# Storing the last four row pairs from partitions 96, 100, 104 and 108, one partition at a time, with sixteen staging slots and x in loads of eight pairs

## The reference

```python
bilinear = jnp.einsum('bie,ied->bid', feature, weight)
out = jnp.einsum('bid,bjd->bij', bilinear, feature)
```

## Time and profile before

| | |
|---|---|
| median of 3 runs | 1463.5 us (1458.56 to 1463.85) |
| the profiled execution's own time | 1465.03 us |
| its span, first to last instruction | 1463.2 us |
| TensorE busy | 1330.3 us (91%) |
| VectorE busy | 985.6 us (67%) |
| ScalarE busy | 934.7 us (64%) |
| moved by DMA | 438.55 MB, mean 300 GB/s |

### The profile page before, as it was taken

One profiled execution on the slowest core, in us unless ns is written; L12 is line 12 of the kernel. 1 busy time (PEld: TensorE's weight loads), 2 busy tenths in 40 slices (PEclk: granted clock), 3 DMA queues, 4 the chain that ended last, 5 costly groups with the idle time before them and its releaser, 6 DMA issues.

```text
span 1463.2 us, 39805 instructions
## 1 busy us (share of the span) xinstructions
PE 1330.3 (91%) x16192; PEld 1225.6 (84%) x16192; DVE 985.6 (67%) x1877; ACT 934.7 (64%) x1100; POOL 306.5 (21%) x518
## 2 busy tenths in 40 slices
PE   7999998999999988998999989999889999999974
PEld 7988888898888888888888878888879888889853
DVE  0667676667666766767676766766676767676785
ACT  5666666666666666766666666666666666666643
POOL 0112122222121212212221212222222222222221
PEclk9999999999999999999999999999999999999998
DMA  9799999999999999999999999999999999999998
GB/s 274 236 301 295 322 313 298 317 285 319 312 286 297 293 308 314 299 322 283 316 304 312 296 292 323 290 314 302 308 312 288 322 304 298 322 300 317 265 262 267
DMA packets 264788, 438.55 MB, mean 300 GB/s; under 512 B 51616, under 2 KB 250272, under 8 KB 252320
## 3 DMA queue, kind: packets, MB, share of 16 engines
q1 hardware_dynamic: 240032, 422.78, 88.9%
q0 software_dynamic: 24576, 13.24, 6.8%
HBM read 108.13 MB, written 327.68 MB: 298 GB/s over the span
## 4 chain that ended last, share of the span: by engine, by line
DMA 42%; PE 34%; SPq 9%; DVE 9%; ACT 3%; issue 3%; ACTq 0%; DVEq 0%; POOLq 0%
DMA out_dram<-staging 42%; PE ps L272 15%; PE ps L256 13%; SPq L194 8%; PE ps L244 6%; DVE staging L305 4%; ACT staging L305 3%; DVE win L357 2%; DVE win L365 1%; DVE win L364 1%; SPq L182 1%; DMA x<-feature_dram 1%; SPq L189 0%; ACT xt L318 0%; ACT bl L328 0%
## 5 line engine op out<-in xcount | busy, mean ns | idle before, releaser
L272 PE MATMUL ps<-win,bl 64*100 64x200 f32 x8192 | 771.2, 338 | 59.4 <-DVE staging L305 41.0
L272 PEld LDWEIGHTS ps<-win,bl 64*100 64x100 f32 x8192 | 697.8, 207 | 120.6 <-issue 64.2
L305 ACT COPY staging<-ps 100x800 f32<-100x800 f32 x683 | 548.2, 829 | 328.9 <-PE ps L272 169.8
L227 POOL DMA_DIRECT2D out_dram<-staging x512 | 305.8, 597 | 1146.1 <-ACT staging L305 910.4
L305 DVE COPY staging<-ps 100x800 f32<-100x800 f32 x341 | 335.2, 983 | 234.2 <-PE ps L272 206.8
L357 DVE COPY win<-xt 128x400 f32<-128x400 f32 x512 | 278.5, 544 | 208.7 <-PE ps L272 155.1
L256 PE MATMUL ps<-xt,w 64*64 64x128 f32 x6400 | 371.0, 271 | 15.2 <-DVE staging L305 9.9
L256 PEld LDWEIGHTS ps<-xt,w 64*64 64x64 f32 x6400 | 348.5, 133 | 33.4 <-issue 20.5
L328 ACT COPY bl<-ps 128x1024 f32<-128x1024 f32 (+1 forms) x208 | 202.3, 981 | 153.7 <-PE ps L256 153.7
L244 PE MATMUL ps<-ident,x 128*128 128x128 f32 x1600 | 205.0, 282 | 44.0 <-DVE staging L305 20.1
L244 PEld LDWEIGHTS ps<-ident,x 128*128 128x128 f32 x1600 | 179.2, 144 | 69.1 <-issue 60.4
## 6 DMA issues: line engine op xcount, KB each, us to landing
out_dram<-staging SPq DMA_DIRECT2D x1024, 300.0 KB, 7.6
x<-feature_dram SPq DMA_DIRECT2D x80, 1024.0 KB, 9.7
x<-feature_dram SPq DMA_DIRECT2D x16, 1280.0 KB, 9.7
out_dram<-staging POOLq DMA_DIRECT2D x512, 25.0 KB, 5.8
w<-weight_dram SPq DMA_DIRECT2D x24, 128.0 KB, 6.0
w<-weight_dram SPq DMA_DIRECT2D x2, 64.0 KB, 4.6
```

The costliest lines, as they stand in the source:

```text
L227: nc.gpsimd.dma_start(out_v[FA:FH, PB * (s - 1):PB * (s + 1), :], staging[FA:FH, slot - 1:slot + 1].rearrange("p s b h j -> p (s b) (h j)" ...
L272: last = nc.tensor.matmul(tile[0:FH, h, F * b:F * (b + 1)], row_of_bl(n, R * k + PB * i + b)[64 * h:64 * h + 64], win[64 * h:64 * h + 64, ...
L305: copy(staging[:, slot, :, :, :].rearrange("p b h j -> p h b j"), tile_of("scores", s)[0:FH, :, 0:PB * F].rearrange("p h (b j) -> p h b j" ...
```

## The change

- **The rest on SyncE.** Pairs 96 to 99 are kept on partitions 96, 100, 104 and 108 (`TOP` is 109, the places between hold zeros, written once by three memsets on VectorE for which ScalarE waits at the start). After every eighth set SyncE issues four transfers, each of one partition x sixteen batches. GpSimd stores nothing more.
- **Sixteen staging slots** in place of ten; the rest's semaphore covers eight slots.
- **x in loads of eight pairs.** Two buffers of one group each, so two buffers hold one bundle where they held two. The loads that go out two sets behind a bundle's transposes are for the very next bundle.
- **Three window slots** in place of four.
- **Seven bundles**, the last of four pairs, slipped in at other sets.
- Scores and staging copies run over 109 partitions in place of 100.

```diff
-    OSLOTS = 10
-    WSLOTS = 4
+    OSLOTS = 16
+    WSLOTS = 3
     FA = FH // 16 * 16
-    BUNDLES = [range(2 * v, 2 * v + 2) for v in range(NG // 2 - 1)] + [range(NG // 2 * 2 - 2, NG)]
+    APART = 4
+    TOP = FA + APART * (FH - FA - 1) + 1
+    REST = 16 // PB
+    BUNDLES = [range(2 * v, min(2 * v + 2, NG)) for v in range((NG + 1) // 2)]
...
-    transposed_at = {3: 0, 9: 1, 19: 2, 29: 3, 40: 4, 50: 5}
-    weighed_at = {9: 0, 19: 1, 29: 2, 40: 3, 50: 4, 59: 5}
+    transposed_at = {3: 0, 10: 1, 19: 2, 28: 3, 37: 4, 46: 5, 54: 6}
+    weighed_at = {10: 0, 19: 1, 28: 2, 37: 3, 46: 4, 54: 5, 59: 6}
...
-        x = sbuf("x", [128, XSLOTS, 2 * E * XPAIRS])
+        x = sbuf("x", [128, XSLOTS, 16 * E])
-        staging = sbuf("staging", [FH, OSLOTS, PB, 2, F])
+        staging = sbuf("staging", [TOP, OSLOTS, PB, 2, F])
...
             def load_x(at):
-                n, v = at // NV, at % NV
+                n, u = at // NG, at % NG
                 if at >= XSLOTS:
-                    before = at - XSLOTS
-                    sp.wait_ge(transposed, before // NV * NG + BUNDLES[before % NV][-1] + 1)
+                    sp.wait_ge(transposed, at - XSLOTS + 1)
...
+            def store_rest(s):
+                first = s - REST + 1
+                half = slice(first % OSLOTS, first % OSLOTS + REST)
+                for i in range(FH - FA):
+                    p = FA + APART * i
+                    sp.dma_start(out_v[FA + i:FA + i + 1, PB * first:PB * (s + 1), :],
+                                 staging[p:p + 1, half].rearrange("p s b h j -> p (s b) (h j)")
+                                 ).then_inc(rest_written[first % OSLOTS // REST], 16)
...
                     store(n * SETS_B + s)
-                    if s - 2 in transposed_at:
-                        at = (n + 1) * NV + transposed_at[s - 2] + XSLOTS
-                        if at < BLOCKS * NV:
-                            load_x(at)
+                    if s % REST == REST - 1:
+                        store_rest(n * SETS_B + s)
+                    if n + 1 < BLOCKS and s - 2 in transposed_at:
+                        for u in BUNDLES[transposed_at[s - 2]]:
+                            if (n + 1) * NG + u + XSLOTS < BLOCKS * NG:
+                                load_x((n + 1) * NG + u + XSLOTS)
...
-            for s in range(1, BLOCKS * SETS_B, 2):
-                store_rest(s)
...
-                        last = nc.tensor.matmul(tile[0:FH, h, F * b:F * (b + 1)],
+                        last = nc.tensor.matmul(tile[0:TOP, h, F * b:F * (b + 1)],
...
-                engine.wait_ge(rest_written[slot // 2], 16 * used)
+                engine.wait_ge(rest_written[slot // REST], 16 * (FH - FA) * used)
...
+            act.wait_ge(margin_zero, 3)
...
+            nc.vector.memset(bl[:, FA:TOP, :], 0.0).then_inc(margin_zero, 1)
+            nc.vector.memset(bl[:, 0:FA, FA:TOP], 0.0).then_inc(margin_zero, 1)
+            nc.vector.memset(bl[:, TOP:NB, FA:TOP], 0.0).then_inc(margin_zero, 1)
```

More of the change, by code:

```diff
@@ L40, in feature_interaction @@
     TILES = 4
-    OSLOTS = 10
-    WSLOTS = 4
+    OSLOTS = 16
+    WSLOTS = 3
     FA = FH // 16 * 16
-    BUNDLES = [range(2 * v, 2 * v + 2) for v in range(NG // 2 - 1)] + [range(NG // 2 * 2 - 2, NG)]
+    APART = 4
+    TOP = FA + APART * (FH - FA - 1) + 1
+    REST = 16 // PB
+    BUNDLES = [range(2 * v, min(2 * v + 2, NG)) for v in range((NG + 1) // 2)]
     NV = len(BUNDLES)
-    XPAIRS = max(sum(GROUPS[u] for u in bundle) for bundle in BUNDLES)
     assert 2 * E == 128 and B % NB == 0 and FH % 8 == C and R == 2 * PB
-    assert PB * F <= 512 and OSLOTS % 2 == 0
+    assert PB * F <= 512 and OSLOTS % REST == 0 and SETS_B % REST == 0 and TOP <= NB
     feature_v = feature.rearrange("b f e -> b (f e)")
@@ L53, in feature_interaction @@
     out_v = out.rearrange("b (m h) j -> m b (h j)", h=2)
-    transposed_at = {3: 0, 9: 1, 19: 2, 29: 3, 40: 4, 50: 5}
-    weighed_at = {9: 0, 19: 1, 29: 2, 40: 3, 50: 4, 59: 5}
+    transposed_at = {3: 0, 10: 1, 19: 2, 28: 3, 37: 4, 46: 5, 54: 6}
+    weighed_at = {10: 0, 19: 1, 28: 2, 37: 3, 46: 4, 54: 5, 59: 6}
     assert sorted(transposed_at.values()) == sorted(weighed_at.values()) == list(range(NV))
     assert all(s // 2 + WSLOTS - 1 >= min(2 * BUNDLES[v][-1] + 1, LINES - 1) for s, v in transposed_at.items())
-    assert all(PB * (s + 1) >= min(8 * BUNDLES[v][-1] + 8, FH) for s, v in weighed_at.items())
+    assert all(PB * (s + 1) >= (8 * BUNDLES[v][-1] + 8 if v + 1 < NV else TOP) for s, v in weighed_at.items())
     uses = []
@@ L115, in feature_interaction @@
         out_written = [sem(f"out_written{i}") for i in range(OSLOTS)]
-        rest_written = [sem(f"rest_written{i}") for i in range(OSLOTS // 2)]
+        rest_written = [sem(f"rest_written{i}") for i in range(OSLOTS // REST)]
+        margin_zero = sem("margin_zero")
         block = ctx.enter_context(nc.Block())
@@ L143, in group_of_bl @@
         def group_of_bl(n, u):
-            if n % 2 == 0:
-                return bl[:, 8 * u:8 * u + GROUPS[u], :]
-            return bl[:, :, 8 * u:8 * u + GROUPS[u]]
+            places = slice(8 * u, 8 * u + GROUPS[u]) if 8 * u < FA else slice(FA, TOP, APART)
+            return bl[:, places, :] if n % 2 == 0 else bl[:, :, places]
         def row_of_bl(n, b):
-            return bl[:, b, 0:FH] if n % 2 else bl[:, 0:FH, b]
+            return bl[:, b, 0:TOP] if n % 2 else bl[:, 0:TOP, b]
         def staged_by_dve(s):
@@ L176, in load_x @@
             def load_x(at):
-                n, v = at // NV, at % NV
+                n, u = at // NG, at % NG
                 if at >= XSLOTS:
-                    before = at - XSLOTS
-                    sp.wait_ge(transposed, before // NV * NG + BUNDLES[before % NV][-1] + 1)
-                first, size = 16 * E * BUNDLES[v][0], 2 * E * sum(GROUPS[u] for u in BUNDLES[v])
+                    sp.wait_ge(transposed, at - XSLOTS + 1)
+                size = 2 * E * GROUPS[u]
                 sp.dma_start(x[:, at % XSLOTS, 0:size],
-                             feature_v[n * NB:(n + 1) * NB, first:first + size]
+                             feature_v[n * NB:(n + 1) * NB, 16 * E * u:16 * E * u + size]
                              ).then_inc(x_loaded[at % XSLOTS], 16)
@@ L195, in store @@
                              ).then_inc(out_written[slot], 16)
[L197 to L201, removed]
+            def store_rest(s):
[6 more added lines that the diff above has]
+                                 ).then_inc(rest_written[first % OSLOTS // REST], 16)
+            for u in range(NG + XSLOTS):
+                load_x(u)
+                if u < NG:
+                    load_w(u)
             for n in range(BLOCKS):
@@ L211, in _ @@
                 sp.wait_ge(out_written[slot], 16 * uses)
-                if slot % 2:
-                    sp.wait_ge(rest_written[slot // 2], 16 * uses)
+                if slot % REST == REST - 1:
+                    sp.wait_ge(rest_written[slot // REST], 16 * (FH - FA) * uses)
         @block.gpsimd
@@ L236, in transposes @@
             def transposes(n, u):
[L237 to L241, removed]
+                at = n * NG + u
+                pe.wait_ge(x_loaded[at % XSLOTS], 16 * (at // XSLOTS + 1))
+                wait_tile(pe, "transposes", at)
                 for c in range(GROUPS[u]):
-                    m = 8 * (u - BUNDLES[v][0]) + c
                     last = nc.tensor.transpose(transpose_tile(n, u)[:, c // C, :, c % C, :],
-                                               x[:, at % XSLOTS, 2 * E * m:2 * E * (m + 1)], ident[:])
+                                               x[:, at % XSLOTS, 2 * E * c:2 * E * (c + 1)], ident[:])
                 last.then_inc(transposed, 1)
@@ L303, in stage @@
                 engine.wait_ge(out_written[slot], 16 * used)
-                engine.wait_ge(rest_written[slot // 2], 16 * used)
+                engine.wait_ge(rest_written[slot // REST], 16 * (FH - FA) * used)
             copy(staging[:, slot, :, :, :].rearrange("p b h j -> p h b j"),
-                 tile_of("scores", s)[0:FH, :, 0:PB * F].rearrange("p h (b j) -> p h b j", j=F)
+                 tile_of("scores", s)[0:TOP, :, 0:PB * F].rearrange("p h (b j) -> p h b j", j=F)
                  ).then_inc(staged, 1)
```

## The result

The changed kernel takes 1839.2 us (median of 4 runs, 1837.0 to 1845.1) against 1461.5 before (median of 4, the three of the first table among them): a ratio of 1.259, 95% interval 1.255 to 1.263. The forecast was 1493 with a range of 1400 to 1560. The direction was right, the size far off: +378 us where +30 were forecast.

A forecast was written before the change was run, and what follows sets the result against it. TensorE and the DMA engines were taken as nearly full together in the overlapped blocks. Fifteen blocks +33, last block -7 and block 0 +4 made +30 on the median of 1463.5: about 1493 us, range 1400 to 1560.

The forecast's parts named there:

- Bounds of the kernel before: Overlapped blocks: TensorE and DMA engines nearly full together; at most 6.3 us a block, 94 us in all, to win.
- a, the load chain: Between bundles' transposes: two sets, a store, then the next bundle's load follow in turn, 12.1 to 13.4 us, taken as 12.8.
- The gaps of the prediction's sum: Sets between bundles' transposes in an overlapped block: together 90.2 us, 91.1 with the rest's charge, against 88.9 before.
- windows and loads hide each other: Gaps of nine sets: the windows' 13.3 us lies above the load chain's 12.8, so the two are not added.
- b, three window slots: Scores after transposes and bilinears wait for VectorE's window copies: nine sets take 13.3 us, 1.2 more than before.
- the prediction's two cases: Gaps of nine sets with three window slots: 13.0 us with no staged set first, 13.9 with one.
- At nothing: SyncE's issues: SyncE's queue: stores, rests and loads issue in 6.6 us of the 11 that eight sets take, so nearly no cost.
- the load of set 39: Overlapped blocks: four rest transfers stand ahead of this load of x, 1 us more on its chain, 0.9 kept.
- Clogged: Rival, chance 0.11: one-partition transfers queue for the same partition, up to 27% of the DMA engines; 1610 to 1760 us.
- faster: Rival, chance 0.29: VectorE and loads keep up, TensorE's 6.3 us waits shrink by half or more; 1410 us, 1362 to 1450.
- The ends: First and last block: block 0 +4 to +5 us from later loads, last block 7 us less, bounds 0 and 15.

The follow-up runs named there:

- the best version: Changed kernel with one-partition, eight-batch rest transfers on GpSimd's queue, four x buffers, twelve staging slots and four window slots: 1423.1 us, 0.974 of the kernel before.
- control: Kernel before with only the changed kernel's seven bundles and their steps, x still in two buffers of a whole bundle: 1464.8 us.

## Why the prediction was wrong

**Bounds of the kernel before.** TensorE's waits of 6.3 us a block were taken as all there was to win, and no run here won more: the best version still waits 2.5.

**a, the load chain: the step that failed.** The loop was named with its links, and the chain of the changed kernel walks it link by link. The term mis-sized is the load, put at 3.5 to 4.7 us. That 3.5 was read for one load of 512 KB, at the shortest landings of the earlier trace rows. But a bundle is two such loads, issued together, and the transposes of its second half need both: 1024 KB, for which the earlier trace rows gave 5.4 at least, and 1.22 for the store ahead. That makes 6.6 and a loop near 15, where 15.2 was measured. In the changed kernel both loads of a bundle have landed 7.05 us after the first's issue in the median (6.0 to 8.9, 89 pairs in the overlapped blocks), the first of them after 5.3. The rows at hand had the answer; halving the load did not halve what a bundle waits for.

The gaps of the prediction's sum, from one bundle's transposes to the next's, can be read from the traces (us, mean of fourteen blocks; the gap of nine sets is the mean of its four):

| gap | forecast | control | three window slots | changed, no rest | changed |
|---|---|---|---|---|---|
| seven sets | 8.8 | 9.8 | 8.4 | 11.3 | 14.7 |
| nine sets | 13.3 | 12.8 | 13.9 | 15.4 | 15.8 |
| eight sets | 12.3 | 11.8 | 13.2 | 14.5 | 17.2 |
| thirteen sets | 15.9 | 15.8 | 16.8 | 16.9 | 17.6 |

Without the rest, the gaps of nine are each 2.1 us over the forecast and those of seven and eight 2.5 and 2.2, together 13 of the 22 us by which the changed kernel's block is over it. That is the load, and by the column before it a smaller part of it the windows.

The prediction then took the larger of two chains, "windows and loads hide each other". Loads alone are +26.9 a block over the control, windows alone +5.2, and both together, with sixteen slots and without the rest, +15.5, so they do not add. That fits taking the larger, but the larger was the loads. That loads alone cost more than both together goes with the clock, 0.89 over that run and 0.98 over the run without the rest; no run tests whether it is the reason.

**The clock.** Not in the prediction. After the wait of 5.87 us the granted clock was 0.50 for the transposes that followed, 1.7 us more for them. Over the whole span transposes are busy for 256.0 us in place of 205.0 and bilinears for 398.6 in place of 371.0, at a mean granted clock of 0.944 in place of 0.993. TensorE's busy time grew from 1330 to 1481 us in all, of which scores, whose rows can hold waits for windows, make 74.

**b, three window slots.** Mechanism right, size short. The gaps above sum to 90.2 in the forecast and to 94.0 with windows alone: 13.9 in the gaps of nine, the upper of the prediction's two cases, where it took 13.3, and 0.9 more in each of the gaps of eight and thirteen.

**At nothing: SyncE's issues.** The second step that failed. Rests were priced at 0.33 us, the shortest issue of a load of x; they take 0.50 at least, 0.59 in the median, and with them in its queue the last block's DMA share is 0.85, without them 0.96. They were charged to the load of set 39 alone, 0.9 us. The table shows where they cost, changed against no rest: most in the gaps of seven and eight, 3.4 and 2.8 us. There the next bundle's first load is issued 9.1 and 13.3 us after the transposes began, in the mean, against 5.2 and 9.7 without the rest and 5.8 and 10.3 with the rest on GpSimd's queue: the loads stand behind the rest and the stores that it delays. The rest's price in the change is 146 us, of which 82 go when its issues leave SyncE's queue; 64 stay.

**The rivals.** "Clogged" came nearest in time, 1610 to 1760, but not by its mechanism: the share of the DMA engines fell, stores land sooner (5.0 us in the median, 7.6 before), and on GpSimd's queue the one-partition shape takes half the DMA engines' time that the old one took, not four times as much. The "faster" rival's slot waits did shrink, from 112.4 to 30.0 us, to no use.

**The ends.** Block 0: +4 taken, +7.5 measured; the loads alone give it +12.9 over the control (59.6 against 46.7), so they can be the reason, but it was not followed. Last block: -7 forecast, +9 measured, by SyncE's issues: with the rest on GpSimd's queue it is 5.9 shorter than before, close to the forecast, and without the rest 12 shorter.

What stays open: with the rest on GpSimd's queue 3.6 us a block and 6.4 in the last block remain over the run without it, and with the rest spread on SyncE's queue (1700.1 us) the last block takes 1.4 us a set where SyncE's issues make 1.2. Neither was traced further. How much of the loss is the clock's was not tested by itself.

## What to carry to other kernels

Halving a buffer moves the load that fills it next to its use: draw the loop of load, compute and release that results, and price its transfer for all the bytes that the consumer waits for, at a landing time under load. Where the loop is longer than the work, two nearly full engines take turns, and over the whole stage neither looks full: 0.82 for TensorE and 0.78 for the DMA engines here. A transfer also costs the queue that issues it, and here by its shape, not its bytes: move small ones to a queue with nothing behind them.

## What the runs showed of the hardware

- One partition x sixteen rows of 1600 bytes held SyncE for 502 ns at least, one partition x eight rows for 620, four partitions x four rows for 266, 96 partitions x two rows for 317. From one partition, half the rows took longer.
- On GpSimd's queue the rest took 99 us of the DMA engines' time as four neighbours x four rows and 54 as one partition x sixteen; as one partition x eight it took 53.
- Partitions 96 to 99 in place of 96, 100, 104 and 108: 1.9% of the whole time, in a single run.
- After 5.87 us without a matmul the granted clock was 0.50 (1.2 GHz), and 16 transposes took 3.67 us against 1.94.
- Two loads of 512 KB, issued together among stores, had both landed 7.05 us after the first's issue in the median (6.0 to 8.9).
